# Seven-product Q projections in their own stage, with a DRAM spill, and transposes of two heads at a time

## The reference, cut to what matters

```python
x = _layernorm(x)                                  # (8, 128, 512); B, S, D
xn = rmsnorm(x) * ln_weight
h_q = (xn @ w_q.T).reshape(b, lq, 32, 128)         # 32 heads of 128
h_k = (ctx @ w_k.T).reshape(b, lk, 32, 128)
h_v = (ctx @ w_v.T).reshape(b, lk, 32, 128)
score = einsum('bqhd,bkhd->bhqk', h_q, h_k) + position_bias
score = softmax(where(mask, score, -inf)); score = where(mask, score, 0)
attn = einsum('bhqk,bkhd->bqhd', score, h_v).reshape(b, lq, 4096)
x = x0 + tanh(g_xattn) * (x + attn @ w_out.T)
# then, on layernorm(x): a base product 512 x 512 plus top-2 of 28 rank-8 experts,
# gated by tanh(g_ffn) and added to x
```

## Time and profile before

| | |
|---|---|
| median of 3 runs | 897.38 us (897.1 to 898.45) |
| the profiled execution | 897.92 us, its span 896.1 us |
| TensorE clock granted | full in all 40 slices |
| busy share of the span | PE 99%, PEld 87%, DVE 71%, ACT 38%, POOL 27% |
| DMA | 46.75 MB, mean 52 GB/s |

### The profile page before, as it was taken

One profiled execution on the slowest core, in us unless ns is written; L12 is line 12 of the kernel. 1 busy time (PEld: TensorE's weight loads), 2 busy tenths in 40 slices (PEclk: granted clock), 3 DMA queues, 4 the chain that ended last, 5 costly groups with the idle time before them and its releaser, 6 DMA issues.

```text
span 896.1 us, 14659 instructions
## 1 busy us (share of the span) xinstructions
PE 884.8 (99%) x5218; PEld 783.0 (87%) x5218; DVE 640.1 (71%) x1650; ACT 340.6 (38%) x879; POOL 240.3 (27%) x110
## 2 busy tenths in 40 slices
PE   8999999999999999999999999999999999999998
PEld 7888888898989889898988989898888989898886
DVE  6887693948678494957759495867849495788863
ACT  4353333433433332433333343333334244344320
POOL 1441424232041423313142322214242320432200
PEclk9999999999999999999999999999999999999999
DMA  9220200202020010202011020202002020212001
GB/s 303 73 101 7 82 18 0 99 0 94 6 94 6 28 72 0 94 6 94 6 56 43 0 99 0 94 6 94 6 11 89 0 94 6 94 48 72 1 24 71
DMA packets 18272, 46.75 MB, mean 52 GB/s; under 512 B 3152, under 2 KB 5200, under 8 KB 18256
## 3 DMA queue, kind: packets, MB, share of 16 engines
q1 hardware_dynamic: 18256, 46.54, 14.8%
HBM read 44.43 MB, written 2.10 MB: 52 GB/s over the span
## 4 chain that ended last, share of the span: by engine, by line
PE 90%; DVE 5%; ACT 1%; DMA 1%; issue 1%; POOL 1%; SPq 1%; ACTq 0%; DVEq 0%; POOLq 0%
PE proj_ps L836 72%; PE score_ps L868 6%; PE pv_ps L894 3%; PE turn_ps L894 3%; PE proj_ps L1120 2%; DVE probs_t L636 2%; PE proj_ps L1138 1%; DMA acc<-in_x 1%; PE pv_ps L836 1%; PE turn_ps L836 1%; POOL root L277 1%; SPq L185 0%; DVE probs L625 0%; ACT w_hi L314 0%; ACT probs L332 0%
## 5 line engine op out<-in xcount | busy, mean ns | idle before, releaser
L636 DVE STREAM_TRANSPOSE probs_t<-probs 32x128 f32<-32x128 f32 x960 | 290.3, 302 | 12.8
L260 POOL TENSOR_TENSOR w_lo<-w_raw,w_hi 128x1024 fp32r<-128x1024 f32 x64 | 152.9, 2411 | 348.1 <-ACT w_hi L314 348.1
L651 DVE TENSOR_TENSOR acc<-proj_ps,acc 128x512 f32<-128x512 f32 x112 | 77.5, 692 | 146.9 <-PE proj_ps L836 146.9
L836 PE MATMUL proj_ps<-w_hi,ct_hi 128*128 128x256 f32 x512 | 147.6, 288 | 1.1 <-ACT kt L319 0.9
L836 PE MATMUL proj_ps<-w_lo,ct_hi 128*128 128x256 f32 x512 | 144.8, 283 | 0.0
L836 PE MATMUL proj_ps<-w_hi,ct_lo 128*128 128x256 f32 x512 | 144.7, 283 | 0.0
L332 ACT ACTIVATE probs<-probs,neg_max 128x128 f32<-128x128 f32 x256 | 99.6, 391 | 110.7 <-DVE neg_max L614 110.6
L271 POOL TENSOR_TENSOR comb<-mask_add,bias_sb 128x1024 f32<-128x1024 f32 x32 | 76.6, 2396 | 210.1 <-DVE probs L611 201.5
L836 PE MATMUL proj_ps<-xt_hi,w_hi 128*128 128x512 f32 x256 | 105.2, 411 | 0.6 <-POOL w_lo L260 0.4
L314 ACT ACTIVATE w_hi<-w_raw 128x1024 fp32r<-128x1024 f32 x65 | 65.2, 1053 | 105.7 <-PE proj_ps L836 105.7
L836 PEld LDWEIGHTS proj_ps<-w_hi,ct_hi 128*128 128x128 f32 x512 | 98.0, 191 | 2.3 <-ACT kt L319 1.3
(11 more groups left out here) (150 smaller groups left out, 1385.2 us busy)
## 6 DMA issues: line engine op xcount, KB each, us to landing
w_raw<-in_weights SPq DMA_DIRECT2D x67, 512.0 KB, 5.7
acc<-in_x SPq DMA_DIRECT2D x4, 512.0 KB, 9.9
bias_sb<-in_bias SPq DMA_DIRECT2D x16, 128.0 KB, 2.0
out<-probs SPq DMA_DIRECT2D x8, 256.0 KB, 2.0
w_raw<-in_x SPq DMA_DIRECT2D x6, 256.0 KB, 2.7
qt<-in_ctx_t SPq DMA_DIRECT2D x4, 256.0 KB, 5.5
kt<-in_ctx_t SPq DMA_DIRECT2D x4, 256.0 KB, 6.4
w_raw<-in_weights SPq DMA_DIRECT2D x2, 256.0 KB, 3.8
```

The costliest lines, as they stand in the source:

```text
L260: pool.tensor_tensor(lo, w_raw[:, k, :], hi.bitcast(F32), ALU.subtract).then_inc(w_lo_done[k], 1)
L636: tr = dve.transpose(probs_t[k:k + Q32, u % 2, :, q:q + Q32], probs[q:q + Q32, u, :, k:k + Q32])
L651: dve.tensor_tensor(acc[:, b, :], proj_ps[b % BANKS][:, :], acc[:, b, :], ALU.add).then_inc(acc_done, 1)
L836: mm = pe.matmul(o, lhs(l, n), rhs(r, n), start=(start and n == 0 and m == 0), stop=(stop and n == terms - 1 and m == 2))
```

## The change

Q of phase 0 is computed as before. Q of phases 1 to 15 moves out of the loop to a new stage of 15 steps ahead of it (i = 0 to 14). There the product of a 256 x 512 weight block (two heads) with the 512 x 1024 activations is seen as 2 x 2 blocks and done by Strassen's seven products (Winograd's form with shared sums): 7 products of 6 matmuls of 512 columns, where `chunk` used 4 x 12. The four sums of activations (T1 to T4) are formed once by DVE (1024 elements a row each) from an unsplit copy `xt_raw`, that ACT makes from PSUM; in every step POOL forms four sums of weights (S1 to S4) of 128x256 and their rests, ACT their leads and those of three plain blocks, DVE three rests (`rest_a`) and five additions of 128x512 (`post`), ACT three PSUM copies. Q then goes to DRAM (`q_spill`) in four stores of 256 KB a step; the loop reads 1 MB of it back in each pass, before the scores. Weights for the next step are loaded once their predecessor has been split.

In the loop, chunks are K (0 to 3) and V (4 to 7) alone, and the order of all engines changes. DVE does all four `add_bias` first, then `normalise` 0 and 1, then turns both heads of half 0 with 16 transposes of 32x256 each, then half 1 likewise; TensorE runs `pv` in pairs. `probs`, `probs_t`, `xt_raw` and the stage's buffers share one tensor. `mask_add` moves from DVE to POOL.

```diff
 TensorE, the new stage
+            def product(o, w, x, start):
+                for c in range(2):
+                    for m, (l, r) in enumerate(((0, 0), (1, 0), (0, 1))):
+                        mm = pe.matmul(o[:, :], w[l][:, c, :], x[r][:, c, :], start=(start and c == 0 and m == 0),
+                                       stop=(c == 1 and m == 2), skip_group_check=not start)
+                mm.then_inc(q_prod, 1)
+            def q_phase(i):
...
+                product(p1_ps, A11, B11, True)
+                product(p5_ps, S1, T1, True)
+                product(p1_ps, A12, B21, False)
+                product(p2_ps, A22, T4, True)
+                product(p6_ps, S2, T2, True)
+                product(p5_ps, S4, B22, False)
+                pe.wait_ge(q_post, i * POSTS + 1)
+                product(p6_ps, S3, T3, False)
 DVE, a step of the new stage
+            def q_phase(i):
+                last = isinstance(i, int) and i == NQ - 1
+                if not last:
+                    rest_a(i + 1, 0, 0, 0)
+                    rest_a(i + 1, 1, 0, 1)
...
+                post(i, 5, t_sum, p6_ps[:, :], s_copy)
+                if not last:
+                    rest_a(i + 1, 2, 1, 1)
+                post(i, 6, q_buf[:, 0, half(1)], p5_ps[:, :], t_sum, 0, 1)
+                post(i, 7, v_sum, p6_ps[:, :], s_copy)
+                post(i, 4, q_buf[:, 1, half(0)], p2_ps[:, :], v_sum, 1, 0)
+                post(i, 2, q_buf[:, 1, half(1)], w_copy, v_sum, 1, 1)
 DVE, ahead of it
+            dve.wait_ge(xt_raw_done, B)
+            t_form(0, b_block(0, 1), b_block(0, 0))
+            dve.wait_ge(t_done, 1)
+            t_form(1, b_block(1, 1), t_raw[0])
+            dve.wait_ge(t_done, 2)
+            t_form(3, b_block(1, 0), t_raw[1])
+            rest_t(0, 1)
+            t_form(2, b_block(1, 1), b_block(0, 1))
+            rest_a(0, 0, 0, 0)
 POOL, ahead of it and in it
             rest(WQ, 0)
+            rest(WK, 1)
+            s_forms(0)
+            rest_s(0, 0, 0)
...
 SP
+            def load_forms(i):
+                sp.wait_ge(qa_lo, i * AF + AF)
+                sp.wait_ge(s_step, i * SF + SF)
+                load_w(WQ, i + 2)
...
+                store_q(i, 0, 0)
+                if not isinstance(i, int) or i < NQ - 1:
+                    load_forms(i + 1)
+                sp.wait_ge(q_post, i * POSTS + 2)
+                store_q(i, 0, 1)
 POOL in the loop: as before, without Q's rest
             with pool.Fori(1, LAST) as p:
-                add_mask(p, False)
-                for k in (WQ, WK, WV):
+                add_mask(p)
+                for k in (WK, WV):
                     rest(k, p + 1)
                 rest(WO, p)
 DVE in the loop
-            def turn_probs(a, u):
-
-                dve.wait_ge(probs_done, a * UNITS + (u + 1))
-                if u >= 2:
-
-                    dve.wait_ge(pv_done, a * UNITS + (u - 1))
+            def turn_probs(a, t):
+
+                dve.wait_ge(probs_done, a * UNITS + (HP * t + HP))
                 for q in range(0, S, Q32):
                     for k in range(0, S, Q32):
-                        tr = dve.transpose(probs_t[k:k + Q32, u % 2, :, q:q + Q32], probs[q:q + Q32, u, :, k:k + Q32])
+                        tr = dve.transpose(probs_t[k:k + Q32, t, :, :, q:q + Q32].rearrange("k j b q -> k (j b) q"),
+                                           probs[q:q + Q32, HP * t:HP * t + HP, :, k:k + Q32].rearrange("q j b k -> q (j b) k"))
                 tr.then_inc(turn_copied, 1)
             def iteration(a):
-                add_bias(a, 0)
-                add_bias(a, 1)
+                for u in range(UNITS):
+                    add_bias(a, u)
                 normalise(a, 0)
+                normalise(a, 1)
                 turn_probs(a, 0)
-                normalise(a, 1)
-                add_bias(a, 2)
+                normalise(a, 2)
+                normalise(a, 3)
+                if isinstance(a, int):
+                    add_bias(a + 1, 0)
+                    add_bias(a + 1, 1)
                 turn_probs(a, 1)
 TensorE in the loop
                 scores(a, 0)
                 scores(a, 1)
+
+                pe.wait_ge(q_copied, NQ * COPIES)
+                pe.wait_ge(q_post, NQ * POSTS)
                 chunk(0)
+                scores(a, 2)
+                scores(a, 3)
                 chunk(1)
-                scores(a, 2)
                 chunk(2)
-                scores(a, 3)
-
-                pe.wait_ge(proj_copied, p * PROJ)
                 chunk(3)
+                chunk(UNITS)
+
+                pe.wait_ge(proj_copied, so_far(p))
                 pv(a, 0)
...
```

More of the change, by code:

```diff
@@ L380, in _ @@
             copy_proj(0, UNITS + 2, 2, v_dst(2))
-            copy_proj(0, UNITS + 3, 0, q_or_k(0))
+            for i in range(G):
+                raw_xt(i)
+            copy_proj(0, UNITS + 3, 0, q_at(0))
             for i in range(G, B):
                 lead_xt(i)
[L384 to L389, removed]
+            copy_proj(0, UNITS + 4, 1, q_at(1))
@@ new lines, in _, with lead_a, lead_s, lead_t @@
+            for i in range(G, B):
+                raw_xt(i)
+            lead(WK, 1)
+            def lead_a(i, n, j, k):
+                act.wait_ge(w_in[WQ], i * 16 + 32)
+                act.activation(columns(w_hi, WQ, n), wq_block(j, k), ACT.Copy).then_inc(qa_hi, 1)
+            def lead_s(i, n):
+                act.wait_ge(s_step, i * SF + (n + 1))
+                act.activation(columns(w_hi, WO, n), columns(w_raw, WO, n), ACT.Copy).then_inc(qs_hi, 1)
+            def lead_t(n):
+                act.wait_ge(t_done, (1, 2, 4, 3)[n])
+                act.activation(tf_hi[:, n, :, :], t_raw[n], ACT.Copy).then_inc(t_hi_done, 1)
@@ new lines, in _, with product, copy_product @@
+            lead_s(0, 0)
+            lead_s(0, 1)
+            lead_s(0, 3)
+            lead_s(0, 2)
+            copy_proj(0, UNITS + 5, 2, q_at(2))
+            lead_t(0)
+            act.wait_ge(proj_done, PROJ0 - 1)
+            lead_a(0, 0, 0, 0)
+            copy_proj(0, UNITS + 6, 0, q_at(3))
+            lead_t(3)
+            lead_a(0, 1, 0, 1)
+            lead_a(0, 2, 1, 1)
+            def product(i, n):
+                act.wait_ge(q_prod, i * PRODUCTS + n)
+            def copy_product(i, dst, ps):
+                act.activation(dst, ps[:, :], ACT.Copy).then_inc(q_copied, 1)
@@ L390, in _ @@
+            q_phase(0)
+            with act.Fori(1, NQ - 1) as i:
+                q_phase(i)
+            q_phase(NQ - 1)
+            lead(WV, 1)
+            product(NQ - 1, 7)
             lead(WO, 0)
+            act.wait_ge(w_in[WQ], 16 * (NPH + 1))
+            act.activation(w_hi[:, WQ, :], w_raw[:, WQ, :], ACT.Copy).then_inc(w_hi_done[WQ], 1)
             def iteration(p):
@@ new lines, in _, with post @@
+            dve.wait_ge(xt_raw_done, B)
[7 more added lines that the diff above has]
+            rest_a(0, 0, 0, 0)
+            rest_a(0, 1, 0, 1)
+            rest_t(1, 3)
+            rest_a(0, 2, 1, 1)
+            rest_t(2, 4)
+            def post(i, n, dst, ps, add, j=None, t=None):
+                dve.wait_ge(q_prod, i * PRODUCTS + n)
+                if j is not None and not (isinstance(i, int) and i == 0):
+                    dve.wait_ge(q_stored[j, t], i * 16)
+                dve.tensor_tensor(dst, ps, add, ALU.add).then_inc(q_post, 1)
```

400 lines of the change are left out of this document (288 added, 112 removed).

## The result

| | before | after |
|---|---|---|
| median | 897.24 us (896.46 to 898.45, 4 runs) | 961.18 us (960.54 to 962.07, 4 runs) |
| ratio | | 1.0712, interval 1.0694 to 1.0731 |
| span of the profiled execution | 896.1 us | 958.7 us |
| mean granted clock | full | 0.966 |

The change costs 64 us. The direction was right and the size wrong: 933 was forecast, with 950 as the upper end. Each ratio in the experiments is taken against executions of the kernel before that were made with that run (medians 898.2 to 898.26); one of these, a slow one of 1798 us, is left out.

What follows compares the result with a forecast made beforehand. TensorE, busy 99% of the span, was taken to bound the kernel. -20.4 - 2.2 + 12 + 4 + 39 + 3 = +35.4 on the profiled 897.9 gave 933.3, median 933; own range 923 to 943, wider range 899 to 950.

Steps and rivals of the forecast that it cites:

- Products, -20.4: In the 15 Q phases, 42 matmuls instead of 48 at 0.227 us each save 20.4 us; a step takes 9.5.
- rival (4): In the new stage the weight-load ring binds: a step takes 10.6 us, +15 in all, 948 us; chance 0.10.
- The loop pass up to the stall: In each pass POOL's additions hold DVE, the first turn ends at 19.9 us, and TensorE stalls 2.6 at `pv`.
- rival (1): In the loop POOL's additions don't hold DVE up: stall 0.3 us a pass, 898 us, level with before; chance 0.20.
- The merged turn, 0.43: In the loop a DVE transpose of 32x256 takes 0.43 us, 7.1 for 16; bounds 5.05 and 10.1.
- Rival (2): In the loop transposes of 256 elements are as cheap as those of 128: stall 0.5 us, 902 us; chance 0.07.
- rival (3): In the loop merged transposes save nothing, 10.1 us a turn: stalls of 5.6 and 1.8, 1005 us; chance 0.06.
- "A pass takes 43.1, and 15 of them +39 us": In the loop a pass takes 43.1 us with TensorE's stall of 2.6, and 15 passes add 39 us.
- The way in, +12: Ahead of the stage's first product 8 us idle, with step 0's waits of 3.5 and 0.3 together +12, bounds 6 and 16.
- The way out, +4: From the stage into the first pass, waits for the last stores, `biased` and the last post cost +4 us (2 to 6).
- The tail, +3 and its stall: After phase 15's scores, copy and `pv` come sooner behind each other without chunks between: +3 us (0 to 5); stall 2.6 a pass.

Runs made afterwards that it cites:

- Run 1: The changed kernel, with POOL's two additions of mask and bias waiting in each pass until both normalises of half 0 are done: 906.49 us, 1.0099 times before.
- run 3: The changed kernel, with each head turned by its own 16 transposes of 32x128 instead of two heads by 16 of 32x256: 981.24 us, 1.0932 times before.
- Run 2: The changed kernel, with ten unused matmuls of 512 columns ahead of `pv(a, 0)` in each pass, filling TensorE's stall: 942.06 us, 1.0494 times before.
- run 4: The changed kernel, with POOL's rest of the K weights of phase 1 moved behind the sums and rests of step 0: 953.51 us, 1.0609 times before.
- Run 6: The changed kernel with the edits of Run 1 and run 4, plus reorderings at the way in and in the tail: 897.62 us, 0.9994 times before.
- run 5: The kernel before, with POOL's additions of mask and bias waiting for the turn of the first half, to meet the normalising: 916.26 us, 1.0199 times before.
- run 7: The kernel of Run 6, with each head turned by its own transposes of 32x128: 912.26 us, 1.0158 times before.
- run 9: The kernel of Run 6, with POOL's K rest behind step 1's rests and ACT's two late `pv` copies ahead of the last exponentials: 893.53 us, 0.9948.

## Why the prediction was wrong

- **Products, -20.4.** Right: a step at full pace takes 9.52 us. DVE's rests in it take 0.58 to 0.98 instead of 0.43, which TensorE doesn't feel. In this trace the weight load's landing is 3.3 us at the median and no later step waits for it, so rival (4) is out.
- **The loop pass up to the stall.** Right in each step: POOL starts at 481.37, 6.38 into the pass (6.42 forecast), L895 is held to 2.85, turns take 7.18, the wait is 2.46 against 2.6. Run 1 shows that POOL is the cause, so rival (1) is out: L354, the former L271, does hold DVE. The Trainium skill ("SBUF — State Buffer", Who interferes with whom) says that a DVE instruction with two SBUF inputs contends with a GpSimd instruction that reads SBUF, and the trace agrees, with 2.85 us against 0.69.
- **The merged turn, 0.43.** Right, at 0.436. Rival (2) is out; for rival (3), run 3 shows that merging saves, though less than the forecast took, since its single turns overlap in pairs.
- **"A pass takes 43.1, and 15 of them +39 us". This is the step that failed.** The length of the stall was right. The step priced it at that length ("a wait put in front of TensorE costs all of itself", and no more), and took the pace behind it to be that of the kernel before. That kernel has the full clock in all its slices, but it also has no idle stretch of this length in the loop, so its rows could not vouch for the pace after one. The measured price is 2.46 of waiting and, in 10 of 13 passes, some 1.5 more at half clock: 44.4 a pass on the mean instead of 43.1, +16.8 in the 13. Run 2 shows it by filling the stall: 19.1 us come back though the wait is as long.
- **The way in, +12.** 14.7, in its bounds; 2.7 of it is half clock behind the idle stretch. The place was right (POOL's K rest ahead of the sums, run 4). The parts were not: idle time 10.5 against 8, and 1.9 in step 0 against 3.8.
- **The way out, +4.** With its stall 8.2 against 6.6. The stores were waited for as said (DVE's first L881 waits 2.34 us for them), TensorE's own wait there is 1.91, and two stretches at half clock, behind it and behind the stall, came on top.
- **The tail, +3 and its stall.** 12.6 against 5.6, the second term that was off. The step named only that copy and `pv` come sooner behind each other. The trace shows four waits of 2.98, 1.21, 2.06 and 1.84, 8.1 in all where the kernel before had 1.4, and three stretches at half clock (2.8 us by run 2). Run 6 took the waits down to 3.4 in all, by order alone.
- **The range.** Its upper end was held by rival (4) and by the bounds of the way in. No case in it let the price of a us of idle be other than one us, so that a stall of the right length still fell 11 us outside.

Open: why 3 of the 13 passes keep their clock after the same stall was not settled. The trace shows that the place of the fall moves from pass to pass: 0.7 and 0.3 us behind the end of the stall, then 0.1 and 0.5 ahead of it, then comes a pass without; then 0.5 behind, at the end, 0.4 ahead, and again one without; and so once more. So the stalls are alike, but not where the fall would come in them. The last 0.37 us of a mended pass (40.87 against the 40.5 of the sum) were not traced either.

## What to carry to other kernels

When work moves from one of DVE and POOL to the other, or its neighbours in time change, list for each POOL operation which DVE instruction with two inputs in SBUF it can now meet; its length is then POOL's and not its own, however small it is. A wait of some 2 us that TensorE gets in a kernel that had none is to be priced with the chance of a stretch at half clock behind it, not at its length alone: here 2.5 us of idle cost 4.0 in 10 of 13 passes. Look for the missing us in the order of the instructions first: one wait on POOL was worth 54.7 us, the other reorderings 13 more (906.49 to 893.53), while the arithmetic that the change saves is worth 20.

## What the runs showed of the hardware that was not expected

- The granted clock fell to half for 3.4 us after waits of 2.46 us in 10 of 13 passes and in 3 not, after one of 1.91 and not after one of 1.89; a stretch in a pass costs some 1.5 us. None followed the waits of 0.76 (run 5) and 1.08 (run 7) in the later passes, nor one of 2.61 in run 9; with waits of 3.42 (run 3) 9 of the 13 passes had one, 4 of them of 6.8 us.
- The Trainium skill ("TensorE: Matmul & The Clock Gate", Part 1) describes the two levels, 1.2 and 2.4 GHz, and that the clock follows how busy TensorE has been. The traces agree: the clock is at full or at half and nothing between (the 0.57 above is a mean over both), and run 2 shows that it follows the idle time.
- DVE transposes of 32x128 came 0.316 us apart when each went to other partitions than its neighbour and 0.255 apart on the mean when pairs shared them; 32x256 takes 0.436 to 0.449. With the earlier trace rows that is some 1.05 ns an element and 0.17 us fixed.
- A DVE product of 128x4 elements was held for 2.24 us by a POOL addition that began 0.17 us before it.
- POOL's additions, laid under DVE's transposes, slowed neither: 4.75 and 7.18 us.
